# Second projection of a Mamba block made with tokens on the partitions: gate and value without transposes of the gated rows

## What is computed

```python
y = y * silu(z)                       # (512, 512), from the selective scan
m = y @ out_proj_w.T                  # (512, 256)
m = gelu(m, approximate=False)
g = m @ glu_w.T + glu_b               # (512, 512)
m = g[..., :256] * sigmoid(g[..., 256:])
x1 = x + (skip + m)                   # then layer norm, router, shared expert, experts
```

## Time and profile before

| | us |
|---|---|
| median of 3 runs | 4408.09 |
| lowest, highest | 4399.77, 4429.23 |
| the profiled execution | 4427.95 |
| its span (first to last instruction) | 4426.0 |

### The profile page before, as it was taken

How to read it: one execution, slowest core, us unless ns; L and a number is a source line. 1 busy time by engine, 2 the same in 40 slices (tenths; PEclk the granted TensorE clock), 3 DMA queues, 4 the chain that set the end, 5 groups by cost and what they waited for, 6 DMA issues and landing times.

```text
span 4426.0 us, 54723 instructions
## 1 busy us (share of the span) xinstructions
PE 3595.1 (81%) x16225; PEld 2345.2 (53%) x16225; DVE 3749.6 (85%) x3725; ACT 3217.2 (73%) x5176; POOL 3953.0 (89%) x1934
## 2 busy tenths in 40 slices
PE   5688888888888888888888888888888888887765
PEld 2455555555555555555555555555555555555454
DVE  3899989898998989898998989899898989999442
ACT  4678777777777777777777777777777777776343
POOL 3999999999999999999999999999999999999266
PEclk7799989998998989898998999899898989998888
DMA  3222312332222222223132222221222322321576
GB/s 126 91 79 77 103 63 95 103 103 98 90 66 100 81 80 103 103 98 102 54 103 71 87 103 103 98 98 65 96 87 71 103 103 98 103 74 36 123 181 133
DMA packets 133560, 415.01 MB, mean 94 GB/s; under 512 B 21592, under 2 KB 80088, under 8 KB 100328
## 3 DMA queue, kind: packets, MB, share of 16 engines
q1 hardware_dynamic: 111720, 358.50, 22.4%
q0 software_dynamic: 21504, 52.44, 6.5%
HBM read 326.88 MB, written 50.46 MB: 85 GB/s over the span
## 4 chain that ended last, share of the span: by engine, by line
POOL 52%; issue 27%; PE 8%; DVE 5%; ACT 3%; DMA 3%; POOLq 1%; DVEq 0%; SPq 0%; ACTq 0%
POOL hs L388 32%; POOL hs L397 15%; POOL dtu L412 3%; DVE ps L1327 2%; PE ps L862 2%; DMA out<-hs,dt 2%; DVE hs L1327 1%; PE ps L978 1%; POOL dt L407 1%; POOL out L472 1%; ACT ps L513 1%; PE ps L906 1%; DMA hs<-table,dt 1%; PE ps L851 1%; PE ps L886 1%
## 5 line engine op out<-in xcount | busy, mean ns | idle before, releaser
L388 POOL TENSOR_TENSOR hs<-dtu,b_all 128x1024 f32<-128x1024 f32 x1024 | 2424.4, 2402 | 47.4 <-PE ps L862 46.3
L513 ACT ACTIVATE ps<-dt,neg_a 128x512 f32<-128x512 f32 x2048 | 1326.0, 683 | 439.6 <-DVE hs L1327 229.3
L1327 DVE TENSOR_TENSOR_SCAN hs<-ps,hs 128x1024 f32<-128x1024 f32 x512 | 1167.6, 2282 | 215.7 <-ACT ps L513 157.0
L862 PEld LDWEIGHTS ps<-ident,hs 128*128 128x128 f32 x8192 | 1040.0, 153 | 522.3 <-issue 407.4
L397 POOL TENSOR_TENSOR hs<-hs,c_all 128x1024 f32<-128x1024 f32 x512 | 1215.1, 2374 | 76.8 <-DVE hs L1327 76.8
L862 PE MATMUL ps<-ident,hs 128*128 128x128 f32 x8192 | 1171.4, 294 | 108.9 <-issue 61.2
L1327 DVE TENSOR_TENSOR_SCAN ps<-ps,hs 128x1024 f32<-128x1024 f32 x512 | 1169.9, 2285 | 74.8 <-ACT ps L513 69.3
L1337 DVE TENSOR_TENSOR hs<-ps,c_all 128x1024 f32<-128x1024 f32 x512 | 626.2, 1223 | 28.9
L970 PE MATMUL ps<-mT,w_sgu 128*128 128x512 f32 x992 | 483.0, 610 | 90.7 <-ACT hid L667 48.1
L886 PE MATMUL ps<-xnT,w_in 128*128 128x512 f32 x512 | 265.9, 645 | 85.7 <-DVE xc L1231 84.2
L1231 DVE SCALAR_TENSOR_TENSOR xc<-ps,cw_sb,xc 128x509 f32<-128x509 f32 (+2 forms) x384 | 285.4, 743 | 35.2 <-ACT xc L570 26.1
(11 more groups left out here) (175 smaller groups left out, 4403.0 us busy)
## 6 DMA issues: line engine op xcount, KB each, us to landing
b_all<-bc SPq DMA_DIRECT2D x128, 1024.0 KB, 6.2
c_all<-bc SPq DMA_DIRECT2D x128, 1024.0 KB, 7.8
dt<-dtu POOLq DMA_DIRECT2D x64, 512.0 KB, 5.2
c_all<-expert_w SPq DMA_DIRECT2D x64, 384.0 KB, 3.9
table<-rows SPq DMA_DIRECT2D x32, 640.0 KB, 3.8
xin<-x SPq DMA_DIRECT2D x32, 512.0 KB, 3.6
out<-mT SPq DMA_DIRECT2D x32, 512.0 KB, 3.7
bc<-xd SPq DMA_DIRECT2D x32, 64.0 KB, 1.6
```

Of the source, the lines that this page charges most:

```text
L388: pool.tensor_tensor(ring(h, hf, n), dtu[:, JH * hf:JH * hf + JH, :], b_all[:, n, :].unsqueeze(1).broadcast_to([P, JH, L]), ALU.mult)\
L513: i = act.activation(state_of(n)[:, k, :], dt[:, j, :], ACT.Exp, scale=neg_a[:, j, n:n + 1])
L862: m = pe.matmul(ybank[:, i, k * P:(k + 1) * P], ring(h, hf, n)[:, k, i * P:(i + 1) * P], ident[:, :], start=False, stop=(n == N - 1), is_t ...
L1327: dve.tensor_tensor_scan(inputs if s in ON_POOL else whole, whole, inputs, 0.0, ALU.mult, ALU.add).then_inc(state_ready, 1)
```

## The change

Gate and value now come out of PE with tokens on the partitions: `mT` tiles are stationary, 256 columns of `w_glu` move, and the bias is added by a matmul with one contraction row, `ones` (1x128) against a row of `b_glu` (1x512). The gate bank is copied by ACT without a bias; DVE multiplies in PSUM, in place, waits for itself, and adds `xs`. The transposes `turn_m` and the separate `add_m` are gone, so the post stage has two units fewer. `moments_x1` moves from step 15 to step 14, and ACT's `sum_x` waits for the second value unit instead of the transposes. In the last sequence's stage four banks hold value and gate of a token tile each.

```diff
-        sg = hid[:, 0:FM, :]
+        sg = hid[:, 0:FM, :].rearrange("p f l -> p (f l)").rearrange("p (i d) -> p i d", i=NT)
...
+        gate_banks = (0, 1, 6, 7)
...
+            pool.memset(ones[:, :], 1.0).then_inc(consts, 1)
...
             def sum_x(p, h):
-                wait(act, post_read, (p - 2) * POST_USES + POST_MT[1] + 1)
+                wait(act, post_read, (p - 2) * POST_USES + POST_V[1] + 1)
...
-            def read_g(q, f):
-                act.wait_ge(post_full, q * POST_USES + POST_G[f] + 1)
-                act.activation(sg[:, f, :], pobank, ACT.Identity, bias=gb_sb[:, FM + f:FM + f + 1])\
-                    .then_inc(post_read, 1)
+            def read_g(q, c):
+                act.wait_ge(post_full, q * POST_USES + POST_G[c] + 1)
+                act.copy(sg[:, 2 * c:2 * c + 2, :], po_tok).then_inc(post_read, 1)
...
-            def project_glu(q, u, half, f):
+            def project_glu(q, u, half, c):
                 pe.wait_ge(gelu_done, q + 1)
                 use_post(q, u)
-                for k in range(FM):
-                    col = (half * FM + f) * P
-                    m = pe.matmul(pobank, w_glu[:, k, col:col + P], mT[:, k, :],
-                                  start=(k == 0), stop=(k == FM - 1))
-                m.then_inc(post_full, 1)
-
-            def turn_m(q, c):
-                use_post(q, POST_MT[c])
+                cols = slice(half * DM, half * DM + DM)
                 for i in range(2):
-                    for f in range(FM):
-                        m = pe.transpose(po_tok[:, i, f * P:(f + 1) * P], sg[:, f, (2 * c + i) * P:(2 * c + i + 1) * P],
-                                         ident[:, :])
+                    t = 2 * c + i
+                    for k in range(FM):
+                        pe.matmul(po_tok[:, i, :], mT[:, k, t * P:(t + 1) * P], w_glu[:, k, cols],
+                                  start=(k == 0), stop=False)
+                    m = pe.matmul(po_tok[:, i, :], ones[:, :], b_glu[:, cols], start=False, stop=True)
                 m.then_inc(post_full, 1)
...
+            for bank in gate_banks:
+                pe.matmul(ps[:, bank, :], ones[:, :], b_glu[:, :], start=True, stop=False)
+            for k in range(FM):
+                pe.wait_ge(end_gelu, k + 1)
+                for t, bank in enumerate(gate_banks):
+                    m = pe.matmul(ps[:, bank, :], mT[:, k, t * P:(t + 1) * P], w_glu[:, k, :],
+                                  start=False, stop=(k == FM - 1))
...
-            def glu(q, f):
-                dve.wait_ge(post_full, q * POST_USES + POST_V[f] + 1)
-                dve.wait_ge(gate_done, q + 1)
-                dve.scalar_tensor_tensor(sg[:, f, :], pobank, gb_sb[:, f:f + 1], sg[:, f, :],
-                                         ALU.add, ALU.mult).then_inc(post_read, 1)
-
-            def add_m(q, h, c):
-                dve.wait_ge(post_full, q * POST_USES + POST_MT[c] + 1)
+            def glu(q, h, c):
+                dve.wait_ge(post_full, q * POST_USES + POST_V[c] + 1)
                 if c == 0:
+                    dve.wait_ge(gate_done, q + 1)
                     dve.wait_ge(xs_ready, q + 1)
+                dve.tensor_tensor(po_tok, po_tok, sg[:, 2 * c:2 * c + 2, :], ALU.mult).then_inc(gated, 1)
+                wait_apart(dve, gated, 2 * q + c + 1)
                 dve.tensor_tensor(x1[:, 2 * c:2 * c + 2, :], po_tok, xs[h][:, 2 * c:2 * c + 2, :], ALU.add)\
                     .then_inc(post_read, 1)
...
-MOMENTS2 = 15
+MOMENTS2 = 14
...
-MT_AT = (13, 13)
```

More of the change, by code:

```diff
@@ L38, with mamba_moe @@
 LEAST = 1e-20
-def mamba_moe(nc, x, vectors, in_wT, conv_w, x_wT, dt_wT, a_log, out_wT, glu_wT, router_w, sgu_w, sdown_w, expert_w, out, counts, table, bc):
+def mamba_moe(nc, x, vectors, in_wT, conv_w, x_wT, dt_wT, a_log, out_wT, glu_wT, glu_row, router_w, sgu_w, sdown_w, expert_w, out, counts, table, bc):
     ctx = ExitStack()
@@ L65, in mamba_moe @@
         w_glu = sb("w_glu", [P, FM, 2 * DM])
+        b_glu = sb("b_glu", [1, 2 * DM])
+        ones = sb("ones", [1, P])
         w_r = sb("w_r", [P, FM, E + 1])
@@ L169, in mamba_moe @@
         pool_readout = sem("pool_readout")
-        summed = sem("summed")
+        summed, gated = sem("summed"), sem("gated")
         y_read = sem("y_read")
@@ L177, in mamba_moe @@
         rows_stored, out_stored, counts_stored = sem("rows_stored"), sem("out_stored"), sem("counts_stored")
[L178 to L179 removed]
+        end_y, end_m, end_g, end_xt, end_r, end_c, end_sg, end_su, end_dn = (
+            sem(f"end_{n}") for n in ("y", "m", "g", "xt", "r", "c", "sg", "su", "dn"))
         yT_act, yT_dve, end_gelu, end_gate, end_glu, end_x1, end_norm, end_x2_act, end_x2_dve, end_lg = (
@@ L808, in _ @@
             act.preload_act_table_set("sigmoid_and_others")
-            for f in range(FM):
-                act.wait_ge(end_g, f + 1)
-                act.activation(sg[:, f, :], ps[:, f, :], ACT.Sigmoid, bias=gb_sb[:, FM + f:FM + f + 1]).then_inc(end_gate, 1)
+            for t, bank in enumerate(gate_banks):
+                act.wait_ge(end_g, t + 1)
+                act.activation(sg[:, t, :], ps[:, bank, DM:2 * DM], ACT.Sigmoid).then_inc(end_gate, 1)
             use_exp_ln()
@@ L1120, in _ @@
                         m.then_inc(end_m, 1)
-            for half, at in ((1, 0), (0, 6)):
-                for k in range(FM):
-                    pe.wait_ge(end_gelu, k + 1)
-                    for f in range(FM):
-                        col = (half * FM + f) * P
-                        m = pe.matmul(ps[:, at + f, :], w_glu[:, k, col:col + P], mT[:, k, :],
-                                      start=(k == 0), stop=(k == FM - 1))
-                        if k == FM - 1:
-                            m.then_inc(end_g if half else end_v, 1)
-            for f in range(FM):
-                pe.wait_ge(end_glu, f + 1)
-            for c in range(2):
-                for i in range(2):
-                    for f in range(FM):
-                        t = 2 * c + i
-                        m = pe.transpose(ps[:, 2 + c, (i * FM + f) * P:(i * FM + f + 1) * P], sg[:, f, t * P:(t + 1) * P],
-                                         ident[:, :])
-                m.then_inc(end_mt, 1)
+            for bank in gate_banks:
+                pe.matmul(ps[:, bank, :], ones[:, :], b_glu[:, :], start=True, stop=False)
+            for k in range(FM):
+                pe.wait_ge(end_gelu, k + 1)
+                for t, bank in enumerate(gate_banks):
+                    m = pe.matmul(ps[:, bank, :], mT[:, k, t * P:(t + 1) * P], w_glu[:, k, :],
+                                  start=False, stop=(k == FM - 1))
+                    if k == FM - 1:
+                        m.then_inc(end_g, 1)
             for f in range(FM):
@@ L1296, in post_at @@
                     if s == V_AT[f] + AFTER_V:
-                        glu(q, f)
-                for c in range(2):
-                    if s == MT_AT[c] + AFTER_MT:
-                        add_m(q, h, c)
+                        glu(q, h, f)
                 if s == MOMENTS2:
@@ L1422, in _ @@
             dve.tensor_copy(yT[:, 3, :], ps[:, 1, :]).then_inc(yT_dve, 1)
-            for f in range(FM):
-                dve.wait_ge(end_v, f + 1)
-                dve.wait_ge(end_gate, f + 1)
-                dve.scalar_tensor_tensor(sg[:, f, :], ps[:, 6 + f, :], gb_sb[:, f:f + 1], sg[:, f, :],
-                                         ALU.add, ALU.mult).then_inc(end_glu, 1)
-            for c in range(2):
-                dve.wait_ge(end_mt, c + 1)
-                dve.tensor_tensor(x1[:, 2 * c:2 * c + 2, :], ps[:, 2 + c, :].rearrange("p (i d) -> p i d", i=2),
-                                  xs[1][:, 2 * c:2 * c + 2, :], ALU.add).then_inc(end_x1, 1)
-            dve.wait_ge(end_x1, 2)
+            for t in range(NT + 1):
+                if t < NT:
+                    part = ps[:, gate_banks[t], 0:DM]
+                    dve.wait_ge(end_gate, t + 1)
+                    dve.tensor_tensor(part, part, sg[:, t, :], ALU.mult).then_inc(end_glu, 1)
+                if t > 0:
+                    dve.wait_ge(end_glu, t)
+                    dve.tensor_tensor(x1[:, t - 1, :], ps[:, gate_banks[t - 1], 0:DM], xs[1][:, t - 1, :], ALU.add)\
+                        .then_inc(end_x1, 1)
+            dve.wait_ge(end_x1, NT)
             moments(ln2, 1, q, x1)
@@ L1489 @@
 ROUTES = 5
-CONSTS, MADE = 5, 2
-LOADS, POST_LOADS = 7, 5
+CONSTS, MADE = 6, 2
+LOADS, POST_LOADS = 7, 6
 CLEARED = 4
@@ L1507 @@
 AFTER_V = 1
-AFTER_MT = 2
 AFTER_XT = 0
```

21 lines of the change are left out of this document (8 added, 13 removed).

## The result

The changed kernel takes 4446.40 us (median of 4 runs, 4445.67 to 4448.32). The kernel before took 4404.97 us in the runs beside it. The ratio is 1.0076, 95% interval 1.0054 to 1.0098: slower by 0.8%, 41 us between the two medians, 33 us by the ratio. The forecast was 4404 us, no change. The measured time is above the 4370 to 4440 us given for the likeliest case and inside the widened range of 4345 to 4455 us; the kernel did move, and not because of the part that was forecast to cost.

The account below looks back on a forecast made before the run. No engine is saturated; handoffs between engines set the time. -6 us over 31 turns and +2 us in the tail make -4 us, 4404 us on the median's scale; range 4370 to 4440, widened 4345 to 4455 us.

Parts of the forecast that it names:

- the likeliest case: Whole kernel: forecast of no change beyond about 1%, chance 0.58, its own range 4370 to 4440 us.
- The gate unit: PE: a unit grows from 1.99 to 2.79 us, +0.8 us, of which the bias records are 0.93 us.
- step 6: Who pays: DVE gains 0.4 us, POOL's delay is mostly absorbed by later waits; -0.2 us per turn, -6 us over 31.
- What it delays: PE's longer gate units move ACT's read, sigmoid and decays, and so DVE's scan 12, by 1.3 us.
- Product and add: DVE: about 0.7 us each plus 0.15 us self-wait; first pair hidden before scan 12, second adds 0.8 us.
- No transposes, the stall: PE: eight transposes, its stall and DVE's 1.21 us wait go; the z projection waits for the fourth convolution instead.
- Moments ahead of the convolution: DVE: moments delay the fourth convolution by 3.9 us in all, hence ACT's silu; POOL's shift comes 1.75 us later.
- state sum 15: PE's sum behind POOL's product of state 15: stays in place; waiting over some tenths of a us would mean rival B.
- rival B: The displaced convolution decides: POOL's +1.75 us is not absorbed, +54 us, 4462 us; chance 0.17.
- The wait of 3.70 us: POOL's idle time at 2110.10 us in the trace, one of the waits expected to absorb its delay.
- The tail: Last turn: 24 PE records in place of 16, with nothing to hide them; +1.7, say +2 us.
- Rival A: The stall was the limiter: POOL's 3.2 us wait shrinks, 37 to 99 us gained, centre 4350 us; chance 0.25.

Follow-up runs that it names:

- e12: Changed kernel with the bias matmul over 128 rows, 127 of them zeros, in place of one row; 4405.22 us, ratio 0.9985.
- e1: Changed kernel with the moments of x1 moved back to the post stage's step 15, behind the fourth convolution; 4452.97 us, ratio 1.0120.
- e3: Changed kernel with POOL's small shift one step later (SHIFT2 = 17 in place of 16); 4401.34 us, ratio 0.9983.
- e14: Changed kernel with the bias matmul over 128 rows (127 zero) and POOL's shift at SHIFT2 = 17 in place of 16; 4355.18 us, ratio 0.9900.
- e4: Kernel before the change with only POOL's small shift one step later (SHIFT2 = 17); 4416.00 us, ratio 1.0029.
- e9: e8 with two tiny one-row matmuls of 2 columns, overwritten afterwards, ahead of each gate or value unit; 4371.23 us, ratio 0.9913.
- e10: e8 with one tiny one-row matmul of 2 columns, overwritten afterwards, ahead of each gate or value unit; 4351.45 us, ratio 0.9874.
- e13: e2 with two tiny one-row matmuls of 2 columns, overwritten afterwards, ahead of each gate or value unit; 4397.57 us, ratio 1.0003.
- e2: Changed kernel without the one-row bias matmuls of gate and value, for all sequences but the last; 4425.85 us, ratio 1.0042.
- e7: Changed kernel with each unit's bias as one 512-column one-row matmul that opens the unit, ahead of the wait for the gelu; 4462.07 us, ratio 1.0103.
- e8: e7 with POOL's small shift one step later as well (SHIFT2 = 17); 4396.81 us, ratio 0.9974.

## Why the prediction was wrong

By its own steps:

1. *The gate unit.* This is the step that failed first; step 6 failed on top of it. The term was 12 records of 0.233 us, 2.79 us, from the shared down projection, whose weights all have 128 rows. Measured: 3.37 us, eight records of 0.265 and four of 0.31. The upper bound of the bias record, 0.233, was no bound, since no row showed a change between weights of 128 rows and of one. With 128-row weights (e12) it takes 2.68 us, the term would have stood, and the kernel takes 4405.22 us, no change. The table of the Trainium skill, "TensorE: Matmul & The Clock Gate", under "Why this matters for your kernels", puts a matmul with 32 contraction rows level with one of 128; it says nothing of one row, and here one row is dearer, 0.31 us a record where the same matmul over 128 rows takes 0.215. The old unit was also taken too long, 1.99 by duration where 1.82 passes from start to start, so the difference was 1.55 us and not 0.8.
2. *What it delays.* The path was right: unit, ACT's read, unit, ACT's read, sigmoid, decays, scan 12. The first unit is 1.55 us longer, the second 1.45 (3.27 for 1.82), and between them the wait of 0.29 us and a little of the state sum go (0.92 us for 1.33): +2.6 us at the end of the second, +2.5 at ACT's read and +2.46 at scan 12; predicted was +1.3.
3. *Product and add.* Right: 0.70 us in PSUM, 0.69 for the add, 0.15 of waiting for itself, which again speaks against the rule of the Trainium skill, "VectorE: DVE Perf Modes", "Rules for kernel authors", by which it would be nothing. The first pair is just hidden, scan 12 follows it at once, and the second adds 0.8 us in the open.
4. *No transposes, the stall.* Right: L940's stall is gone and the z projection waits 5.4 us for the convolution.
5. *Moments ahead of the convolution.* Its sizes were right and its mechanism wrong. The convolution is late by 5.05 us: 2.46 from step 2 and 2.59 of its own, where 2.65 was predicted. But the silu isn't set by it. ACT's decays of step 16 come 3.24 us later (24.87 against 21.63 us behind the gelu), which is 2.46 and the open 0.8 us of step 3, and the silu follows them without a break. e1 shows it: with the convolution 1.7 us early the silu stays where it was. The shift came 2.86 us late, not 1.75.
6. *Who pays.* Two thirds of POOL's delay were absorbed, 42.1 of 62.6 us, by the very waits named; the rest was not. The place named, state sum 15, was only a small part of it (0.66 us), though by the prediction's own sign more than some tenths there spoke for rival B. The larger one is the state sum ahead of the shared down projection, 47.7 us behind the shift: in the trace of before POOL's product ended there 0.06 us before PE came (2079.93 and 2079.99 us), a margin of nothing that was overlooked, and POOL has no idle time on the way. POOL's product and PE's state sum there, before the change:

```profile
2077.58 2.35 POOL L397 TENSOR_TENSOR hs<-hs,c_all 128x1024 f32<-128x1024 f32 x1
```

```profile
2079.99 1.09 PE L862 MATMUL ps<-ident,hs 128*128 128x128 f32 x8
```

   The wait of 3.70 us that the forecast counted on lies behind this point, and PE sets its end. In POOL's timelines of before and after:

```profile
2110.10 2.36 POOL L388 TENSOR_TENSOR hs<-dtu,b_all 128x1024 f32<-128x1024 f32 x1 [3.70 <-PE ps L862]
```

```profile
2113.76 2.38 POOL L393 TENSOR_TENSOR hs<-dtu,b_all 128x1024 f32<-128x1024 f32 x1 [1.83 <-PE ps L866]
```

   POOL made up 1.9 us there, but PE had its delay by then. e3 shows this to be the path: with the shift a step later PE no longer waits, and 45 us return. This step fails with a unit of the forecast's length too: e12 keeps 91.0 us of that wait, and the later shift (e14) takes 50 us more off it. So that e12 meets the forecast of no change is in part luck: to judge by e14's shorter turns (121.2 us, and 123.7 in e12), the delay that was thought absorbed costs about what the turns gained elsewhere.
7. *The tail.* +2.3 us from PE's first bias matmul to the aggregates (4131.56 to 4145.71, 14.15 us, against 11.88 before), predicted +1.7 to +2.

So rival B's outcome came (POOL's delay not absorbed), about two thirds of its price, by another cause than its own. Rival A's premise fell with e4: the 3.2 us were slack. But A was right that a cheap bias can leave a gain: with 128-row weights and the shift at step 17 the kernel is 1% faster than before.

What the prediction had no term for is PE's gap at the branch. The changed kernel was lucky in it, 5.0 us against 6.7; the shorter turns are some 2.1 us longer than before, the longer ones 1.0 us shorter. Without this luck the change would have cost some 22 us more; that is an estimate, 1.7 us in each of the 13 gaps counted.

The gap is PE's wait for its instructions, as far as the profiles can tell: all 221 stalls end 1.2 to 1.8 us behind a landed packet of q8, and instructions which compute nothing took the long gaps from two packets to one (e9, e10, e13). In all, q8 moved 161 packets in the kernel before, 162 after, 164 in e2 and 175 in e7 and e8, and 162 or 163 in e9, e10 and e13. Open is what decides when the packet starts, which makes the rest of the difference: it begins 1.90 us behind the start of the count matmul in the shown branch of the kernel before and 0.80 us in that of the changed one. Also open is why 92 executions of the kernel before spread over 59 us; the four of the changed one spread over 3, those of e3 over 14.

## What to carry to other kernels

When a unit gets matmuls of another weight height, look at the weight load, not only at the matmul: a one-row bias between 128-row weights cost 0.33 us of lost overlap at each change, and padding it with zero rows to 128 made it cheaper. A wait on an engine is slack or not by what follows it: walk the engine behind the wait until it next idles, and check the margin of every consumer on the way, also of the ones far behind. And before a variant is given up for a few tenths of a per cent, look at what PE does at the loop's branch and at how many packets of the instruction queue land there: some 5 us a pass came and went with the position of the instructions here.

## What the runs showed of the hardware

- Weights of 128 rows and of one row in turn: 0.33 us of idle weight load at each change, 0.31 us per 256-column record of the one-row matmul, 0.215 per record of the same matmul over 128 rows (e12).
- PE idles some 3 to 11 us at the loop's branch (2.95 us in the changed kernel's, 10.75 in e8's shown above). In all 16 kernels these stalls end 1.2 to 1.8 us after a 16384-byte packet of the instruction queue has landed, and the long ones take two packets (e2, e7, e8). Short matmuls that only move the instructions behind them shortened it from 11.0 to 6.3 or 5.9 us (e9, e10) and from 9.1 to 5.3 us (e13).
- An in-place product of 128x512 in PSUM takes 0.70 us, as one that writes SBUF.
